# Three 64-byte gaps in SBUF between the operand tiles of a LayerNorm, attention and FFN kernel

## The chip, the cores and the metric

The kernel runs on one core of one Trainium2 chip. The metric is the device time of one launch in microseconds (us). The engines are named as the profile names them: PE is TensorE's matmul side, PEld its loading of the stationary operand, DVE is VectorE, ACT is ScalarE, POOL is GpSimd, and SPq is the queue of SyncE, from which all transfers are issued.

## What is computed

The input x is 16 x 1024 x 256 in float32. It is normalised over its last dimension (no scale, no shift), and two branches are added to x:

```python
xn = _layernorm(x, axis=-1)
x = x + attention(xn, Wqkv, Wout) + ffn(xn, W1, b1, W2, b2)
# attention: 16 heads of 16; segments of 512 tokens; every 8th token is a key (64 keys);
#   scores minus their maximum over each block of 64 queries, exp,
#   num = w @ v, den = sum(w) + 1e-10, out = num / den, then @ Wout.T
# ffn: relu(xn @ W1 + b1) @ W2 + b2, inner width 1024
```

## The kernel before

The 16 x 1024 tokens are 32 segments of 512. The program is software pipelined: while the hidden layer of segment s is computed, the queries, keys and scores of segments s+1 and s+2 are made. Each engine has its own instruction stream, and a loop over 14 pairs of segments stands between written-out first and last steps.

To keep float32 accuracy with fp32r products, each operand is split in a high and a low part, and `three_products` (L990 to L996) adds hi x hi, lo x hi and hi x lo in PSUM. Each of the three is a pair of a load of the stationary operand (128 x 128) and a product that streams a moving operand of 128 partitions by 512 columns of 4 bytes. Three such products are made for each of the following, in every segment unless it is said otherwise.

- `first_product`: stationary a slice of `w1_hi`/`w1_lo`, moving `xt_hi`/`xt_lo` (normalised x, transposed), output `h_bank`: 8 slices of the inner width times 2 halves of the depth, so 48 products.
- `second_product`: stationary `w2_hi`/`w2_lo`, moving `h_hi`/`h_lo`, output `y_bank`: 48 products. In the very last segment the roles are exchanged (stationary a slice of h, moving 256 columns of w2).
- `queries`: stationary `wq`, moving `xt`: 12 products.
- `output_product`: stationary `wout`, moving `att_hi`/`att_lo`: 12 products.
- `keys_values`: stationary `xkey_hi`/`xkey_lo`, moving `wkv`: 6 products for each pair of segments.

Outside `three_products` there are three more kinds. `scores` (L1063) makes one product for each of 8 pairs of heads, stationary `k_pack`, moving `q_pack`, 96 partitions. `weighted_values` (L1159) makes 32 small ones, stationary `v` (64 partitions by 32 columns), moving `w_exp` (512 columns); eight of them lie side by side in the array. The transposes have `xn_keys`, `kv` or `xn` as stationary and `identity` as moving operand, 128 columns.

The streams of the other engines follow PE. ACT and DVE take PSUM out and split it (ACT writes `h_hi` and `h_full` at L603 and L605, `xt_hi` at L642; DVE writes `xt_lo`, `q_lo` and the shifted scores), POOL makes `h_lo` (L524) and `att_lo`. SP issues all transfers in one fixed order: among others the blocks of x to memory and back (L421, L427), the outputs to memory and back (L438, L444), the keys to memory (L354, L357) and back in `k_pack` (L364), the queries in `q_pack` (L372 waits for `q_lo`, L374 issues). The first `scores` of a segment waits for `q_pack` and `k_pack`.

The tiles are laid out in SBUF in the order in which `sb(...)` is called, each starting at the next multiple of 32 bytes of a partition. In this layout the start of every operand of the products above leaves the remainder 96 when divided by 128: the weights (`w1_hi` starts at byte 35552), `xt` (99296), `xkey`, `q_hi`, `v` (144352), `k_pack` (150496), `q_pack` (125920), `w_exp` (154848), `att_hi` and `h_hi` (204512), and also `xn`, `xn_keys` and `kv`. The one exception is `identity` (16512), with the remainder 0. Slices inside the tiles start at multiples of 128 bytes from there. `y_mem` is the last tile and ends at byte 229088 of the 229376 of a partition.

Of the kernel before, what the change touches and what calls it, by code (L numbers as in the profile page):

```python
# [22 lines left out]
F32 = mybir.dt.float32  # L23
# [5 lines left out]
P = 128  # L29
# [19 lines left out]
def ln_attention_ffn(nc, x, wq_t, wkv_t, wout_t, w1, b1, w2, b2, out):  # L49
# [19 lines left out]
    with ExitStack() as ctx:  # L69
        def sb(name, shape, dt):  # L70
            return ctx.enter_context(nc.sbuf_tensor(name, shape, dt))
# [15 lines left out]
        w1s = [sb(f"w1_{n}", [P, DH, INTER], F32R) for n in ("hi", "lo")]  # L87
        w2s = [sb(f"w2_{n}", [P, NH, D], F32R) for n in ("hi", "lo")]

        x_raw = sb("x_raw", [P, 2, T, D], F32)  # L90
        x_keys = sb("x_keys", [P, D], F32)
        x_b2 = sb("x_b2", [P, 2, T, D], F32)
# [16 lines left out]
        v = sb("v", [P, 2, PAIRS, PW], F32)  # L109
        k_full = sb("k_full", [P, 2, DH, P], F32)  # L110
        k_part = [sb(f"k_{n}", [P, DH, P], F32R) for n in ("hi", "lo")]
        k_pack = sb("k_pack", [P, PAIRS // 2, DH, P], F32R)
        k_dram = nc.dram_tensor("k_dram", [2, PAIRS // 2, PW, DH * P], F32).ap()
        s_max = sb("s_max", [P, PAIRS, NB], F32)
# [5 lines left out]
        den_dram = nc.dram_tensor("den_dram", [P // PW, 2, QUADS, SEG], F32).ap()  # L120
        rden_dram = nc.dram_tensor("rden_dram", [P // PW, 2, QUADS, SEG], F32).ap()
        att = sb("att", [P, QUADS, SEG], F32)
        att_part = [sb(f"att_{n}", [P, QUADS, SEG], F32R) for n in ("hi", "lo")]
        h_full = sb("h_full", [P, HBUF, SEG], F32)
        h_part = [sb(f"h_{n}", [P, HBUF, SEG], F32R) for n in ("hi", "lo")]
# [1141 lines left out]
```

## Time and profile before

| what | us |
|---|---|
| median of 3 runs | 1087.76 |
| lowest and highest of them | 1080.11 and 1087.91 |
| the profiled execution | 1080.21 |
| its span, first to last instruction | 1078.4 |

The profiled execution is one launch on the chip; its own time is 1.8 us above its span, and it lies at the low end of the runs. Durations and starts of instructions are taken from it. Busy time of PE counts overlapping products once, and since products are pipelined one in the row is shown longer (0.39 us) than the distance to the next one (about 0.23 us). The distance between starts is what a product costs.

### The profile page before, as it was taken

The numbers are of one execution on the slowest core, as the hardware profiler recorded it, in microseconds if no ns is written. First come the engines' busy times: TensorE is split into PE (matmuls) and PEld (weight loads), VectorE is DVE, ScalarE is ACT, GpSimd is POOL, SyncE is SP. The second block draws the span as 40 slices with busy tenths as digits, with TensorE's granted clock in tenths as the row PEclk, the third lists the DMA queues.
The fourth block names the chain that finished last, engine by engine and source line by source line (L and its number), as shares of the span: only waits on it lengthen the run. The fifth ranks groups of instructions, "written<-read, shape, count | busy, mean of one in ns | idle before, by whom it ended". The sixth has DMA issues, their size and how long they took to land.

```text
span 1078.4 us, 19171 instructions
## 1 busy us (share of the span) xinstructions
PE 1047.4 (97%) x5381; PEld 813.1 (75%) x5381; DVE 818.8 (76%) x1464; ACT 647.9 (60%) x1080; POOL 622.7 (58%) x487
## 2 busy tenths in 40 slices
PE   5899999999999999999999999999999999999996
PEld 4577787777787777787777787777787777777775
DVE  7787877877877877877877777877877877878632
ACT  5656665666666566665656656566665666655651
POOL 5255565656565665565655655665565656556562
PEclk9999999999999999999999999999999999999999
DMA  5357777787877777777687887777777787866733
GB/s 190 97 154 206 221 210 212 191 233 197 234 223 192 199 214 219 225 213 209 185 234 197 231 224 191 197 215 219 221 209 217 186 229 199 242 192 182 192 108 117
DMA packets 153287, 216.37 MB, mean 201 GB/s; under 512 B 27312, under 2 KB 96432, under 8 KB 153264
## 3 DMA queue, kind: packets, MB, share of 16 engines
q1 hardware_dynamic: 153264, 216.09, 72.3%
q8 instruction: 12, 0.20, 0.1%
q14 instruction: 11, 0.09, 0.0%
HBM read 100.41 MB, written 58.46 MB: 147 GB/s over the span
## 4 chain that ended last, share of the span: by engine, by line
PE 86%; DMA 6%; DVE 3%; SPq 3%; issue 2%; ACT 1%; POOL 0%; POOLq 0%; DVEq 0%; ACTq 0%
PE h_bank L994 36%; PE y_bank L994 36%; PE s_banks L1063 5%; PE misc L1159 3%; PE s_banks L1159 2%; PE misc L994 2%; DMA k_dram<-k_lo 2%; DMA yt_dram<-y_mem 1%; SPq L399 1%; DVE xn L805 1%; DMA xt_dram<-z 1%; DMA k_pack<-k_dram 1%; SPq L438 1%; DVE s_max L822 0%; SPq L421 0%
## 5 line engine op out<-in xcount | busy, mean ns | idle before, releaser
L524 POOL TENSOR_TENSOR h_lo<-h_full,h_hi 128x512 fp32r<-128x512 f32 x256 | 335.8, 1312 | 394.0 <-ACT h_full L605 384.0
L611 ACT ACTIVATE w_exp<-w_exp 128x512 f32<-128x512 f32 x256 | 161.5, 632 | 245.8 <-DVE w_exp L828 243.9
L603 ACT ACTIVATE h_hi<-h_bank,b_cols 128x512 fp32r<-128x512 f32 x256 | 174.5, 682 | 71.2 <-PE h_bank L994 63.9
L994 PE MATMUL h_bank<-xt_hi,w_hi 128*128 128x512 f32 x512 | 206.9, 404 | 0.0
L994 PE MATMUL h_bank<-xt_lo,w_hi 128*128 128x512 f32 x512 | 200.7, 392 | 0.0
L994 PE MATMUL h_bank<-xt_hi,w_lo 128*128 128x512 f32 x512 | 200.2, 391 | 0.0
L994 PE MATMUL y_bank<-h_hi,w_hi 128*128 128x512 f32 x496 | 194.9, 393 | 1.6 <-ACT w_exp L611 1.6
L822 DVE TENSOR_REDUCE s_max<-s_banks 128x8 f32<-128x512 f32 x254 | 170.9, 673 | 33.2 <-PE s_banks L1063 33.0
L994 PE MATMUL y_bank<-h_lo,w_hi 128*128 128x512 f32 x496 | 194.0, 391 | 0.0
L994 PE MATMUL y_bank<-h_hi,w_lo 128*128 128x512 f32 x496 | 193.7, 391 | 0.0
L828 DVE TENSOR_TENSOR w_exp<-s_banks,s_max 128x512 f32<-128x512 f32 x254 | 175.7, 692 | 11.0
L605 ACT ACTIVATE h_full<-h_bank,b_cols 128x512 f32<-128x512 f32 x256 | 174.4, 681 | 0.0
L994 PEld LDWEIGHTS h_bank<-xt_hi,w_hi 128*128 128x128 f32 x512 | 96.2, 188 | 47.2 <-issue 27.1
L994 PEld LDWEIGHTS h_bank<-xt_hi,w_lo 128*128 128x128 f32 x512 | 96.4, 188 | 21.0
L994 PEld LDWEIGHTS y_bank<-h_hi,w_hi 128*128 128x128 f32 x496 | 93.6, 189 | 22.2 <-issue 2.0
L994 PEld LDWEIGHTS h_bank<-xt_lo,w_hi 128*128 128x128 f32 x512 | 96.6, 189 | 17.9
L994 PEld LDWEIGHTS y_bank<-h_lo,w_hi 128*128 128x128 f32 x496 | 93.7, 189 | 20.5
L994 PEld LDWEIGHTS y_bank<-h_hi,w_lo 128*128 128x128 f32 x496 | 93.2, 188 | 20.6
L941 DVE STREAM_TRANSPOSE y_mem<-y_bank 128x512 f32<-128x512 f32 x62 | 44.4, 717 | 77.8 <-PE y_bank L994 77.8
L1063 PE MATMUL s_banks<-q_pack,k_pack 96*128 96x512 f32 x248 | 95.2, 404 | 3.3 <-DMA k_pack<-k_dram 1.6
L536 POOL TENSOR_TENSOR att_lo<-att,att_hi 128x512 fp32r<-128x512 f32 x62 | 78.7, 1290 | 23.8 <-ACT att_hi L616 23.7
L531 POOL TENSOR_TENSOR att<-num_den,rden_rows 128x512 f32<-128x512 f32 x62 | 84.3, 1382 | 5.3 <-DMA rden_rows<-rden_dram 4.8
(135 smaller groups left out, 1513.5 us busy)
## 6 DMA issues: line engine op xcount, KB each, us to landing
q_pack<-q_hi SPq DMA_DIRECT2D x248, 128.0 KB, 2.5
x_raw<-x SPq DMA_DIRECT2D x32, 512.0 KB, 4.8
rden_rows<-rden_dram SPq DMA_DIRECT2D x128, 128.0 KB, 4.6
x_b<-x SPq DMA_DIRECT2D x32, 512.0 KB, 4.5
q_pack<-q_lo SPq DMA_DIRECT2D x124, 128.0 KB, 2.4
yt_dram<-y_mem SPq DMA_DIRECT2D x124, 128.0 KB, 3.6
y_mem<-yt_dram SPq DMA_DIRECT2D x31, 512.0 KB, 4.6
out<-x_b SPq DMA_DIRECT2D x31, 512.0 KB, 3.1
```

What stands on the lines that cost most here:

```text
L524: pool.tensor_tensor(h_part[1][:, i % HBUF], h_full[:, i % HBUF], f32(h_part[0][:, i % HBUF]), ALU.subtract).then_inc(h_lo, 1)
L531: pool.tensor_tensor(att[:, quad], num_den[:, quad, 0], rden_rows[:, quad], ALU.mult).then_inc(att_ready, 1)
L536: pool.tensor_tensor(att_part[1][:, quad], att[:, quad], f32(att_part[0][:, quad]), ALU.subtract).then_inc(att_lo, 1)
L603: act.activation(h_part[0][:, i % HBUF], h_bank[i % 2][:], ACT.Relu, bias=b1_cols[:, i:i + 1]).then_inc(h_hi, 1)
L605: act.activation(h_full[:, i % HBUF], h_bank[i % 2][:], ACT.Relu, bias=b1_cols[:, i:i + 1]).then_inc(h_ready, 1)
L611: act.activation(w_exp[:, pair], w_exp[:, pair], ACT.Exp).then_inc(w_ready, 1)
L822: dve.tensor_reduce(s_max[:, pair], ps.rearrange("p t n i -> p n t i"), AX.XY, ALU.max).then_inc(max_ready, 1)
L828: dve.tensor_tensor(w_exp[:, pair].rearrange("p (t n i) -> p t n i", t=T, n=NB), ps, top, ALU.subtract).then_inc(s_shifted, 1)
L941: dve.transpose(y_blocks[:, :, a].rearrange("p i t n -> p t i n"), y_bank[a][:].rearrange("p (t i n) -> p t i n", t=T, n=PW)).then_inc(y_r ...
L994: mm = pe.matmul(ps, stationary[a], moving[b], start=start and c == 0 and n == 0, stop=stop and c == len(pairs) - 1 and n == 2, skip_group ...
L1063: pe.matmul(s_bank[n % 2], k_pack[0:PR, pair % (PAIRS // 2), pair // (PAIRS // 2)], q_pack[0:PR, pair], start=True, stop=True).then_inc(s_ ...
L1159: mm = pe.matmul(pv_banks[quad][PW * j:PW * (j + 1), a], v[rows, 1 - par, pair], w_exp[rows, pair], start=True, stop=True)
```

## The change

Three tiles of 16 floats (64 bytes in each partition) that nothing reads or writes are put between others. All tiles behind the first gap move up by 64 bytes, those behind the second by 128, those behind the third by 192. No instruction is added, removed or moved.

```diff
         w2s = [sb(f"w2_{n}", [P, NH, D], F32R) for n in ("hi", "lo")]
 
+        sb("gap_weights", [P, 16], F32)
         x_raw = sb("x_raw", [P, 2, T, D], F32)
...
         k_part = [sb(f"k_{n}", [P, DH, P], F32R) for n in ("hi", "lo")]
+        sb("gap_keys", [P, 16], F32)
         k_pack = sb("k_pack", [P, PAIRS // 2, DH, P], F32R)
...
         att = sb("att", [P, QUADS, SEG], F32)
+        sb("gap_rows", [P, 16], F32)
         att_part = [sb(f"att_{n}", [P, QUADS, SEG], F32R) for n in ("hi", "lo")]
```

The remainders by 128 become: weights 96 as before; from `x_raw` to `k_lo` (so `xt`, `xkey`, `q_hi`, `q_pack`, `kv`, `v`, `xn`, `xn_keys`) 32; from `k_pack` to `att` (so `k_pack`, `w_exp`) 96; from `att_hi` on (`att_hi`, `h_full`, `h_hi`, `h_lo`, `y_mem`) 32; `identity` stays at 0. The last byte used becomes 229280.

## Rows read from the trace of the kernel before

**Rows 1.** Head of the page: span and busy time of each engine
```profile
span 1078.4 us, 19171 instructions
...
PE 1047.4 (97%) x5381; PEld 813.1 (75%) x5381; DVE 818.8 (76%) x1464; ACT 647.9 (60%) x1080; POOL 622.7 (58%) x487
```

**Rows 2.** The chain that ended last: share of the span by engine
```profile
PE 86%; DMA 6%; DVE 3%; SPq 3%; issue 2%; ACT 1%; POOL 0%; POOLq 0%; DVEq 0%; ACTq 0%
```

**Rows 3.** Groups of PE: form, count | busy us, mean ns | idle before
```profile
L994 PE MATMUL h_bank<-xt_hi,w_hi 128*128 128x512 f32 x512 | 206.9, 404 | 0.0
...
L994 PE MATMUL y_bank<-h_hi,w_hi 128*128 128x512 f32 x496 | 194.9, 393 | 1.6 <-ACT w_exp L611 1.6
...
L1063 PE MATMUL s_banks<-q_pack,k_pack 96*128 96x512 f32 x248 | 95.2, 404 | 3.3 <-DMA k_pack<-k_dram 1.6 <-DVE w_exp L828 1.0 <-DMA q_pack<-q_hi 0.5
L994 PE MATMUL h_bank<-xt_hi,wq_hi 128*128 128x512 f32 x124 | 48.7, 392 | 0.1
...
L994 PE MATMUL y_bank<-att_hi,wout_hi 128*128 128x512 f32 x124 | 48.2, 389 | 0.0
...
L994 PE MATMUL misc<-wkv_hi,xkey_hi 128*128 128x512 f32 x30 | 11.8, 392 | 1.6 <-issue 1.6
```

**Rows 4.** Stretch of the full pipeline: us, busy (count), PEclk, DMA share, GB/s
```profile
35.00:1040.00 1005.00, 996.20 (x5101) 770.94 (x5099) 780.77 (x1389) 615.65 (x1031) 590.46 (x458) 1.00 0.75 206
```

**Rows 5.** Timeline of PE in mid-span: start us, us, line, operation, out<-in
```profile
521.63 0.39 PE L994 MATMUL h_bank<-xt_lo,w_hi 128*128 128x512 f32 x1
...
525.26 0.39 PE L994 MATMUL y_bank<-att_hi,wout_lo 128*128 128x512 f32 x1
```

**Rows 6.** Timeline of PE from a scores product on
```profile
530.13 0.40 PE L1063 MATMUL s_banks<-q_pack,k_pack 96*128 96x512 f32 x1
530.37 0.40 PE L994 MATMUL y_bank<-h_hi,w_hi 128*128 128x512 f32 x1
530.60 0.40 PE L994 MATMUL y_bank<-h_lo,w_hi 128*128 128x512 f32 x1
530.84 0.39 PE L994 MATMUL y_bank<-h_hi,w_lo 128*128 128x512 f32 x1
531.07 0.39 PE L994 MATMUL y_bank<-h_hi,w_hi 128*128 128x512 f32 x1
531.29 0.39 PE L994 MATMUL y_bank<-h_lo,w_hi 128*128 128x512 f32 x1
```

**Rows 7.** Granted clock of a stretch, PE and PEld in it
```profile
48.00:51.00 3.00, 3.00 (x9) 2.32 (x8) 2.96 (x8) 1.01 (x3) 0.00 (x0) 0.50 0.93 201
```
```profile
48.28 0.63 PE L994 MATMUL h_bank<-xt_lo,w_hi 128*128 128x512 f32 x1
...
50.84 0.63 PE L994 MATMUL y_bank<-h_hi,w_hi 128*128 128x512 f32 x1
```
```profile
49.14 0.33 PEld L994 LDWEIGHTS h_bank<-xt_lo,w_hi 128*128 128x128 f32 x1
```

**Rows 8.** PEld beside the stretch of rows 5
```profile
522.77 0.19 PEld L994 LDWEIGHTS y_bank<-att_lo,wout_hi 128*128 128x128 f32 x1
523.00 0.19 PEld L994 LDWEIGHTS y_bank<-att_hi,wout_lo 128*128 128x128 f32 x1
```

**Rows 9.** Timeline of PE: two sets of the weighted values
```profile
518.49 0.64 PE L1159 MATMUL misc<-w_exp,v 64*32 64x512 f32 x8
518.92 1.06 PE L1159 MATMUL s_banks<-w_exp,v 64*32 64x512 f32 x16
```

**Rows 10.** Waits of PE and of the queue: us in total, times, longest
```profile
PE s_banks L1063 <- DMA k_pack<-k_dram: 1.6, 3, 1.0
```
```profile
SPq L372 <- DVE q_lo L871: 43.9, 31, 3.4
```

**Rows 11.** Last segment, 256 columns moving: timeline of PE
```profile
1044.88 0.28 PE L994 MATMUL y_bank<-w_hi,h_hi 128*128 128x256 f32 x1
...
1045.85 0.28 PE L994 MATMUL y_bank<-w_hi,h_lo 128*128 128x256 f32 x1
```

## The prediction

> **What bounds the kernel now.** I read the head of the page first: PE is busy 97% of the span, DVE 76%, all others less [rows 1]. The chain that ended last is PE for 86% [rows 2], and in the 1005 us of the full pipeline PE is busy 996 us at the full granted clock [rows 4]. So PE sets the time, and the idle time before its groups is a few us in all [rows 3]. The change adds no instruction; it can act only through how fast the same instructions run. The question is whether a product takes longer than its columns need, and whether that surplus depends on where the operands lie.
>
> The timeline answers the first half. In mid-span 16 distances between starts, which cross three kinds of products, take 525.26 - 521.63 = 3.63 us, so 226.9 ns each [rows 5]. What the same 512 columns need is shown by a stretch in which the clock is granted at half, the lower of the two levels (1.2 instead of 2.4 GHz): six distances take 50.84 - 48.28 = 2.56 us, so 426.7 ns [rows 7]. Half of that is 213.3 ns. At full clock each product thus carries a surplus of 13.5 ns that the half clock does not show, though in both a load of 128 columns runs beside it: 0.33 us at half clock [rows 7], 0.19 us at full clock [rows 8]. A fixed cost of exchanging the stationary operand in array cycles would have doubled at half clock; it is gone. A surplus that appears only when the moving operand is read at full pace, with a second read of SBUF beside it, looks like the two reads getting in each other's way.
>
> Two further places speak for a surplus that depends on how the two reads stand to one another. With 256 moving columns eight distances take 1045.85 - 1044.88 = 0.97 us, 121 ns, against 106.7 for the columns alone, so about the same surplus of 14 ns for a product of half the length [rows 11]: it goes with the load, which is the same, not with the columns. And after every scores product (96 partitions instead of 128) four distances take 531.07 - 530.13 = 0.94 us, 235 ns each, before they fall back to 0.22 or 0.23 [rows 6]; the instructions are of the same form as those of rows 5, with the same remainder 96. The same pair of reads can cost 13 or 22 ns, so something about their relative position counts. That it is the address by 128 bytes is what no row shows: all these products have operands of the same remainder.
>
> **The change part by part.** The gaps themselves cost nothing: no instruction touches them, and the last tile still ends inside the partition. Since each gap is 64 bytes and the tiles start at multiples of 32, starts by 64 bytes are what they were; I take the price for transfers and for DVE, ACT and POOL as 0. They are off PE's path (76, 60 and 58% busy, [rows 1]); bounds are plus or minus 1% of the 1005 us if they did react, since DVE at 76% hides more than that.
>
> All three gaps have one effect on PE, so they are summed together. Full-width products: three each of the forms with 512, 496, 124, 124 and 30, and 248 scores, so 3 x 1286 + 248 = 4106 [rows 3]. Their surplus now: 4106 x 13.5 ns = 55.4 us, and four distances after each of the 248 scores by a further 8 ns (235 - 226.9), 7.9 us. Together 63 us of the 1080.2 us depend on how the reads meet.
>
> What is left of it with operands half of 128 bytes apart is unknown; I bound it from both sides. The low end is nothing left, -63 us, by the half-clock distance [rows 7]. The high end is the position shown after scores, 235 ns for all: the 4106 - 992 = 3114 products that are not there yet pay 8 ns more, +25 us [rows 6]. The nearest row for products whose two reads do not meet at full pace is that of the weighted values, where eight tiles of 32 columns share the array and stream 512 columns in 518.92 - 518.49 = 0.43 us [rows 9], 3 ns above 426.7. I take 3 ns as what stays of a product, so the gain is 63 - 4106 x 3 ns = 63 - 12 = 51 us.
>
> The Trainium skill gives a price for that remainder (TensorE: Matmul & The Clock Gate, "Wait — 56ns, not 53.3ns?"): about 2.5 ns a product at full clock, 215.7 ns for 512 columns. The trace's 226.9 ns disagrees with it by 11 ns for these 4-byte operands; by the page the gain would be about 53 us.
>
> Not all of it arrives. 51 us over 31 segments is 1.6 us a segment. SP waits for the low part of the queries 43.9 us over 31 times, so 1.4 us in the mean [rows 10]: that is the slack of the queue ahead of the copies that the next scores need, and the same place already stops PE three times, 1.6 us together. Beyond the slack PE waits for the queue: 31 x (1.6 - 1.4) = 6, with the uneven slack I take 7 us. It would be late as the first scores of a segment waiting for `k_pack`, not for `q_pack`. Bounds: 0 if the queue gets earlier with PE, since much of what it waits for is PE's work; 20 us if in every second segment, the ones that repack keys, over 1 us is lost.
>
> Transposes keep a stationary operand that is not a multiple of 128 away from `identity` (96 before, 32 after), and the score products of the very first segment have both operands at 32; together below 1 us, at 0. The weighted values also get opposite halves, but already run within 3 ns of their columns: 0.
>
> Sum: 1080.2 - 51 + 7 = 1036 us. This is against the profiled execution, which is at the low end of the three runs (median 1087.8); other runs after the change may read up to 7 us more.
>
> **The rivals.**
>
> *Nothing happens.* The surplus belongs to the pair of reads whatever their addresses, for example because a load takes turns at a read path which the moving operand fills only at full clock. For it: the stretch of rows 5 crosses three kinds of products, whose operands lie kilobytes apart, at one even distance, so higher address bits do not matter and the low ones may not either [rows 5]. Against it: the 235 ns after scores. Time: 1080 to 1088 us. The Trainium skill speaks against the change here (TensorE: Matmul & The Clock Gate, step 1 of "Step-by-step: what each phase is for"): loading the next tile's weights does not take read bandwidth from the running product. This trace contradicts it as far as time goes, since 13.5 ns go somewhere, but the rule would leave the change at 1080.
>
> *Part of it.* The moving read covers 2048 bytes a product and the load 512, at different pace, so the one overtakes the other's place by 128 bytes several times wherever they start. Another start saves only some of the meetings: half of the 55 us, 27 us, with no give-back below the slack: 1053 us.
>
> *Slower.* The present alignment is the good one. In steady state the distances fall back to 226.9 by themselves after each disturbance, so this is a settled state, and the disturbed one costs 235. If opposite halves put every pair permanently in the disturbed position, all 4106 products run at 235 ns: 1080 + 25 = 1105 us. It decides at `three_products`, and from the point at which the distance in the stretch of rows 5 exceeds 229.5 ns (11 us of 4106 products) it is slower than 1%.
>
> **How the numbers follow.** The full removal 0.36, part of it 0.13, nothing 0.29, slower 0.22. A measurement of this kernel tells about 1% (11 us) from no change. Faster by over 1% is the first two, 0.49; same 0.29; slower 0.22. The likeliest one's own range is 1017 (nothing left) to 1056 (the 51 us with 20 us given back and the 7 us of spread). The range of all has to take in part of it and nothing as well, up to 1095 with a little of the slower case; it leaves out most of the 0.22. Below, full removal with no give-back is 1017; I put 1019.
>
> **What would show it.** Right: the distance in the stretch of rows 5 falls to 213 to 218 ns, the disturbance after scores to under 4 ns, the half-clock distance stays 426.7, PEld's mean stays near 188 ns, DVE's share rises to about 79%, and waits of scores for `k_pack` appear in more than three segments. If the distance is still 226.9 the first rival holds; at 218 to 224 the second; at 230 or more the third. Wrong in another way: the distances fall and the span does not, with the waits of PE grown by as much; or the distances of one form change and of others not, which would mean that it is not the halves of 128 bytes that count but another address bit.

## The result, and the profile after

The kernel with the gaps takes 1093.15 us (median of 9 runs, 1092.10 to 1096.98), the kernel before 1084.63 us (median of 9, 1080.11 to 1087.91). The ratio is 1.0096, with a 95% interval of 1.0078 to 1.0114. The gaps make the kernel about 1% slower, where 4 to 5% faster was forecast. The profiled execution took 1092.1 us, with a span of 1090.3 us, 11.9 us longer than that of [rows 1]; the mean granted clocks of the two are 0.995 and 0.997. The clock is not the reason: the mean granted clock of these nine runs is 0.990 to 0.995, and that of the 57 runs of the kernel before that stand beside the experiments is 0.987 to 0.995.

The head of the page of the changed kernel, and the shares of its chain:

```profile
span 1090.3 us, 19171 instructions
...
PE 1060.4 (97%) x5381; PEld 814.5 (75%) x5381; DVE 815.9 (75%) x1464; ACT 649.0 (60%) x1080; POOL 622.3 (57%) x487
...
PE 93%; DVE 2%; issue 2%; DMA 2%; SPq 1%; POOL 1%; ACT 0%; POOLq 0%; DVEq 0%; ACTq 0%
```

The instructions are as many as before, and DVE, ACT and POOL are busy for the same time as in [rows 1], within 0.4%. Only PE has more busy time, by 1060.4 - 1047.4 = 13.0 us, and its share of the chain is larger than in [rows 2]. What of the span PE is not busy has not grown: 29.9 us, where it was 31.0. So PE waits no more than before; PE itself is slower. One view says this without a sum: a stretch in which PE is never idle. The same 200 us of mid-span, first of the kernel before, then of the changed one (columns: stretch, us; busy us and count of PE, PEld, DVE, ACT, POOL; granted clock; DMA share; GB/s):

```profile
300.00:500.00 200.00, 200.00 (x1020) 155.97 (x1019) 157.37 (x283) 123.72 (x208) 118.32 (x93) 1.00 0.77 211
```
```profile
300.00:500.00 200.00, 200.00 (x1009) 154.07 (x1008) 153.83 (x277) 121.17 (x203) 119.14 (x94) 1.00 0.72 207
```

PE is busy for all 200 us in both, at the full granted clock, and the gaps leave it 1009 recorded products where it had 1020: 1.1% fewer. The busy share cannot show such a loss; the count can, roughly, since a trace can lack some records.

The timeline of the changed kernel in the place of [rows 5] shows which products pay. First six distances of the first FFN product, then eleven of the output product:

```profile
526.59 0.39 PE L997 MATMUL h_bank<-xt_hi,w_lo 128*128 128x512 f32 x1
...
527.96 0.39 PE L997 MATMUL h_bank<-xt_hi,w_lo 128*128 128x512 f32 x1
528.19 0.40 PE L997 MATMUL y_bank<-att_hi,wout_hi 128*128 128x512 f32 x1
...
530.76 0.39 PE L997 MATMUL y_bank<-att_hi,wout_lo 128*128 128x512 f32 x1
```

With `xt` moving the distance is (527.96 - 526.59) / 6 = 228 ns, with `att_hi` moving it is (530.76 - 528.19) / 11 = 234 ns, and before both were at 226.9 ns [rows 5]. Both pairs lie half of 128 bytes apart, yet they differ. What tells them apart is the sign, an inference here that the experiments take up: `xt` starts 64 bytes above the weights (by the remainder), `att_hi` 64 bytes below them, counted as 160 against 224 in remainders of 256.

After a scores product, in the place of [rows 6]:

```profile
535.62 0.40 PE L1066 MATMUL s_banks<-q_pack,k_pack 96*128 96x512 f32 x1
535.85 0.40 PE L997 MATMUL y_bank<-h_hi,w_hi 128*128 128x512 f32 x1
...
536.55 0.39 PE L997 MATMUL y_bank<-h_hi,w_hi 128*128 128x512 f32 x1
```

Four distances take 0.93 us, 232.5 ns each. These products run at that level now anyway, so the disturbance of [rows 6] is no longer an extra cost.

Where the clock is granted at half, nothing has changed:

```profile
47.75 0.63 PE L997 MATMUL h_bank<-xt_lo,w_hi 128*128 128x512 f32 x1
...
50.31 0.63 PE L997 MATMUL y_bank<-h_hi,w_hi 128*128 128x512 f32 x1
```

Six distances take 2.56 us as in [rows 7], 426.7 ns each. The waits of PE for the keys, in the place of [rows 10]:

```profile
PE s_banks L1066 <- DMA k_pack<-k_dram: 1.0, 1, 1.0
```

One wait instead of three, which fits a slower PE that gives the queue more time. The starts of all recorded products of 512 columns, taken together, account for the loss. What the distances between 212 and 245 ns have above 213.3 ns sums up to 61.1 us before and 74.1 us after. That is 13.0 us more, as much as PE's busy time has grown; the span is 11.9 us longer.

### The profile page after: what moved, and what is told of

Its sections match the earlier page's. It is cut to its first block, busy times and chain, and to the rows that moved or that the text cites. A ratio compares the mean times of both kernels' runs of the same rounds, so it can differ in the third digit from the quotient of the medians.

```text
span 1090.3 us, 19171 instructions
## 1 busy us (share of the span) xinstructions
PE 1060.4 (97%) x5381; PEld 814.5 (75%) x5381; DVE 815.9 (75%) x1464; ACT 649.0 (60%) x1080; POOL 622.3 (57%) x487
## 4 chain that ended last, share of the span: by engine, by line
PE 93%; DVE 2%; issue 2%; DMA 2%; SPq 1%; POOL 1%; ACT 0%; POOLq 0%; DVEq 0%; ACTq 0%
PE h_bank L997 40%; PE y_bank L997 39%; PE s_banks L1066 5%; PE misc L1162 3%; PE s_banks L1162 2%; PE misc L997 2%; DVE xn L808 0%; DMA k_dram<-k_lo 0%; DMA yt_dram<-y_mem 0%; DMA x_raw<-x 0%; PE misc L1128 0%; PE misc L1111 0%; SPq L402 0%; PE s_banks L1077 0%; DMA xt_dram<-z 0%
```

## The experiments

Theory one: the surplus of a product depends on the distance between the starts of its moving and stationary operand, and the kernel before had the best one, zero. Its rivals: the surplus depends on where each operand starts by itself; it has to do with other tiles that the gaps moved, read by DVE, ACT, POOL or DMAs; it goes with the volume of the stationary load. A second question was the period: 128 bytes, as the prediction thought, or another. The expectations give their theories letters of their own, explained there. The three kernels with products alone ran once each, the others in several rounds beside the kernel before, whose medians in them are 1083.94, 1084.68 and 1084.07 us.

**The products alone, one pair of starts after the other.** The whole computation is left out; 24 products follow each other for each pair of starts, and nothing else runs.

```diff
+for g, (_, m, s, n) in enumerate(groups()):
+    for r in range(24):
+        mm = pe.matmul(banks[g % 2][:, 0:n], stat[:, s:s + P], mov[:, m:m + n], start=True, stop=True)
```

> A kernel of fp32r products alone, 24 in a row for each pair of starts: the moving operand is shifted by 4 to 512 bytes against a fixed stationary one, then both together by 16 to 112 bytes, then the stationary one alone, then with 384, 320 and 256 columns. It leaves out the whole computation. Theory A (the distance of two starts depends on moving start minus stationary start, modulo 128): the distance goes from 226.7 ns at 0 to about 233 ns at 64 bytes and comes back at 128, 256 and 384; shifting both together changes nothing. Theory B (the sum goes by the absolute place of one operand): shifting both by 64 gives 233 ns too, and shifting only the stationary one differs from the mirror image. Theory C (address makes no difference to PE and something else in the kernel slowed it): 226.7 ns everywhere. If some shift reaches 213 to 216 ns there is a layout that beats both kernels.

The timeline of this kernel; each row is one group of 24 products, so the start of the next group less its own start, divided by 24, is the distance. The groups are shifts of the moving operand of 0, 4, 20, 28, 64, 128 and 192 bytes, each shown with the row behind it, then the stationary operand alone by 64 bytes, and 256 columns at 0:

```profile
24.30 5.60 PE L71 MATMUL bankb<-mov,stat 128*128 128x512 f32 x24
29.74 5.84 PE L71 MATMUL banka<-mov,stat 128*128 128x512 f32 x24
35.41 5.75 PE L71 MATMUL bankb<-mov,stat 128*128 128x512 f32 x24
...
52.06 5.92 PE L71 MATMUL banka<-mov,stat 128*128 128x512 f32 x24
57.81 5.77 PE L71 MATMUL bankb<-mov,stat 128*128 128x512 f32 x24
63.42 5.60 PE L71 MATMUL banka<-mov,stat 128*128 128x512 f32 x24
68.86 5.76 PE L71 MATMUL bankb<-mov,stat 128*128 128x512 f32 x24
...
113.45 5.66 PE L71 MATMUL bankb<-mov,stat 128*128 128x512 f32 x24
118.94 5.83 PE L71 MATMUL banka<-mov,stat 128*128 128x512 f32 x24
...
202.78 5.76 PE L71 MATMUL bankb<-mov,stat 128*128 128x512 f32 x24
208.38 5.76 PE L71 MATMUL banka<-mov,stat 128*128 128x512 f32 x24
...
225.19 5.75 PE L71 MATMUL bankb<-mov,stat 128*128 128x512 f32 x24
230.78 5.79 PE L71 MATMUL banka<-mov,stat 128*128 128x512 f32 x24
...
391.74 5.76 PE L71 MATMUL bankb<-mov,stat 128*128 128x512 f32 x24
397.34 5.77 PE L71 MATMUL banka<-mov,stat 128*128 128x512 f32 x24
...
418.31 3.04 PE L71 MATMUL bankb<-mov,stat 128*128 128x256 f32 x24
421.18 2.99 PE L71 MATMUL banka<-mov,stat 128*128 128x256 f32 x24
```

Read from these rows: 5.44 / 24 = 226.7 ns at 0, 236 at 4 bytes, 240 at 20, 227 at 28, 228.8 at +64, 233.3 at 128, 233 at 192. The settled distances (the mean of the last twelve of each group) in a table, in ns:

| moving start less stationary start, bytes | 0 | 4 | 8 | 12 | 16 | 20 | 24 | 28 | 32 | 64 | 96 | 128 | 160 | 192 | 240 | 256 |
|---|---|---|---|---|---|---|---|---|---|---|---|---|---|---|---|---|
| distance | 226.7 | 236.7 | 233.3 | 228.9 | 231.7 | 240.0 | 233.3 | 226.7 | 233.3 | 228.8 | 233.3 | 233.3 | 234.3 | 233.3 | 226.7 | 226.7 |

Shifts of 272, 320 and 384 bytes give the same as 16, 64 and 128 within 1 ns: the period is 256 bytes, and theory A of the expectation, with 128, is wrong in its period. No shift is below 226.7. Both operands shifted together by 32, 64 or 96 bytes stay at 226.7, and the stationary operand alone shifted by 64 gives 5.60 / 24 = 233.3, the value of -64 (192 in the table). So for a stationary start at a multiple of 32 bytes, as all tiles here have, it is the difference that counts, and its sign too. At finer steps the difference is not all: shifts of both by an odd multiple of 16 give 230.0, and in the second kernel of this kind a stationary start 16 bytes off gives another table, with 226.7 at a difference of 64 and 228.8 at 192. With 256 columns the distance is 2.87 / 24 = 120 ns: the surplus is again about 13 ns.

**One gap in front of everything.** All operands move by 64 bytes, their differences stay.

```diff
+sb("gap_front", [P, 16], F32)
 identity = sb("identity", [P, P], F32)
```

> One gap of 64 bytes in front of all tiles, so that every operand moves by 64 bytes and no difference between operands changes (remainder 32 for all, identity 64). Theory A: same as before, ratio 1.000 within 0.003, distances of 226.7 ns in the stretch of rows 5. Theory B: slower, as after, ratio 1.007 to 1.012.

Ratio 1.0004 (0.9974 to 1.0033), median 1083.71 us, and the sum of the distances above 213.3 ns is 60.8 us, beside 61.1 before. Where the tiles lie by themselves does not matter at this step of 64 bytes, within 0.3% for the whole kernel and 0.3 us for PE's distances. The rival of single places is out. The rival of other tiles loses its ground too: the products alone show the same distances with nothing else running, and the busy times of the other engines did not grow with the gaps.

**The third gap alone.** Only `att` and `h` parts move against the weights, by +64 bytes.

```diff
+sb("gap_rows", [P, 16], F32)
 att_part = ...
```

> Only the third gap (64 bytes before the halves of the attention rows): att, h_hi, h_lo lie opposite the weights, xt, queries, keys and values as before. Theory A: only the second product and the output product (60 of 131 full-width products of a segment) rise to about 233 ns and the first product and the queries stay at 226.7 except next to them; 31 segments x 60 x 6.6 ns = 12 us more minus what the disturbed products after scores cost already: ratio 1.004 to 1.010. Theory D (only the keys, queries and scores matter, through the gaps at the keys): ratio 1.000.

Ratio 1.0032 (1.0013 to 1.0051), median 1088.45 us. By the table 3 x (496 + 124) = 1860 products pay 2.1 ns, an estimate of 4 us; the medians differ by 4.5, less than the 0.4 to 1.0% that was expected from 233 ns. The sum of the distances grows by 6.1 us. The products of `h` and `att` stand at 230.5 ns in the mean, above the 228.8 of the table, and those of `xt`, whose starts have not changed and which stand between them, rise from 227.8 to 229.0 ns in the mean: a product's distance depends on its neighbours as well.

**The gaps at 32, 96 and 32 bytes.** `xt` against the weights gets +32, `h` and `att` get 160, both poor in the table.

```diff
-sb("gap_weights", [P, 16], F32)
+sb("gap_weights", [P, 8], F32)
...
-sb("gap_keys", [P, 16], F32)
+sb("gap_keys", [P, 24], F32)
...
-sb("gap_rows", [P, 16], F32)
+sb("gap_rows", [P, 8], F32)
```

> The same three places, with gaps of 32, 96 and 32 bytes: moving minus stationary is 32 instead of 64 bytes (modulo 128). If the cost grows with the distance of the halves, between before and after: ratio 1.003 to 1.008. If 128 bytes are eight places of 16 and each shift has a settled state of its own, anything from 0.96 to 1.03; the scan at 32 bytes tells which, and the kernel must follow it: each ns of the distance is 4.1 us.

Ratio 1.0136 (1.0114 to 1.0159), median 1099.22 us, slower than the change, and the sum of the distances is 19.9 us above that of the kernel before. By the table 1908 products at 6.6 ns and 1950 at 7.6 ns would pay 27 us, less some 7 us that the products behind scores paid already, so about 20, an estimate. The loss follows the table.

**One gap of 128 bytes behind the weights.** If the period were 128 bytes, nothing would change.

```diff
+sb("gap_weights", [P, 32], F32)
 x_raw = ...
```

> One gap of 128 bytes behind the weights: all remainders by 128 are as in the kernel before, those by 256 differ by 128 between weights and moving operands. Theory M128 (the difference counts modulo 128, as the change supposes): ratio 1.000. Theory M256 (it counts modulo 256, as in the scan, 233.3 ns at 128): 3858 products outside the scores pay 6.7 ns more, 26 us, minus up to 7 us of disturbance that is in that level already: ratio 1.016 to 1.025.

Ratio 1.0131 (1.0105 to 1.0156), median 1098.37 us. The timeline of this kernel, eleven distances of the output product:

```profile
533.56 0.40 PE L995 MATMUL y_bank<-att_hi,wout_hi 128*128 128x512 f32 x1
...
536.13 0.40 PE L995 MATMUL y_bank<-att_hi,wout_lo 128*128 128x512 f32 x1
```

2.57 / 11 = 234 ns, the value of the scan at 128. The period of 128 bytes is out. The loss is below the 1.6 to 2.5% that was expected, and less than the table alone gives: 3858 products by 6.6 ns are 25 us. The four products behind each scores product already paid their 8 ns before [rows 6], which takes off 992 x 6.6 ns = 6.5 us; the sum of the distances has grown by 15.7 us, and what is missing to 19 stays open.

**The first gap alone.** The products of `xt`, `h` and `att` all get +64. Of the full-width products only those of the keys and values, 90 in all, get -64, since `wkv` lies in front of the gap; the scores keep 0.

```diff
+sb("gap_weights", [P, 16], F32)
 x_raw = ...
```

> The first gap alone (64 bytes behind the weights): moving minus stationary is +64 bytes in the first and second product, queries and output product, where the change has +64 for xt and -64 for h and att. By the scan +64 costs 228.8 ns and -64 (192) 233.3 ns: 3858 x 2.2 ns = 8 us, less the part that hides in the disturbance after scores: ratio 1.003 to 1.008, so faster than the change (1.0096). If the sign doesn't count, the same as the change or more: 1.010 or above.

Ratio 1.0051 (1.0031 to 1.0072), median 1089.95 us: about half of the change's loss, although here too every operand of `three_products` lies half of 128 bytes from its partner. The sum of the distances grows by 5.8 us instead of 13.0. The sign that the two levels of the changed kernel's timeline suggested is confirmed by the total.

**The products alone in other forms.** The whole computation is left out again; each group varies one property at shift 0 unless it is said otherwise.

```diff
-mm = pe.matmul(banks[g % 2][:, 0:n], stat[:, s:s + P], mov[:, m:m + n], start=True, stop=True)
+mm = pe.matmul(banks[g % 2][0:cols, 0:n], w, x_, start=True, stop=True)
```

> Products alone again, 24 in a row for each form; the whole computation is left out. Theory F (the surplus over 213.3 ns is the load's read of SBUF meeting the moving read): with 96, 64 and 32 stationary columns the surplus of 13.3 ns shrinks in proportion to about 10, 7 and 3 ns; with the stationary operand read from one element only (step 0) or the moving one from one element only it changes and no longer depends on the start; bf16 operands, half the bytes, come near 215 to 217 ns at any shift. Theory G (the surplus is a fixed cost of an fp32r product): 13.3 ns in all of these. Theory H (96 partitions disturb): one product of 96 partitions among 11 of 128 gives 232.5, 237.5, 232.5, 231 ns behind it and then 226.7, and all of 96 partitions in a row give 226.7. The shifts repeat the scan: 228.8 at 64 bytes, 233.3 at 128 and 192, 226.7 at 256, 233.3 at 384, 233.3 at 768 minus a multiple of 256 and so on; with the stationary start 16 bytes off, another table of the same kind, nowhere below 226.

The timeline of this kernel, with 96, 64 and 32 stationary columns, 96 and 64 partitions, then a moving operand of step 0 (one column read over and over), both operands of step 0, and bf16 at shift 64:

```profile
20.64 5.69 PE L97 MATMUL banka<-mov,stat 128*96 128x512 f32 x24
26.17 5.68 PE L97 MATMUL bankb<-mov,stat 128*64 128x512 f32 x24
31.68 5.72 PE L97 MATMUL banka<-mov,stat 128*32 128x512 f32 x24
37.24 5.62 PE L97 MATMUL bankb<-mov,stat 96*128 96x512 f32 x24
42.80 5.75 PE L97 MATMUL banka<-mov,stat 64*128 64x512 f32 x24
...
88.39 5.41 PE L97 MATMUL bankb<-mov,stat 128*128 128x512 f32 x24
93.63 5.41 PE L97 MATMUL banka<-mov,stat 128*128 128x512 f32 x24
...
104.08 5.34 PE L97 MATMUL banka<-mov_b,stat_b 128*128 128x512 bf16 x24
109.26 5.34 PE L97 MATMUL bankb<-mov_b,stat_b 128*128 128x512 bf16 x23
```

A load of a quarter of the columns does not shrink the surplus; the settled distance even rises, to 231.7 ns with 32 columns. The rival of the load's volume is out. A moving operand of step 0 takes 5.24 / 24 = 218 ns, while a stationary operand of step 0 with a normal moving one takes 231.7: some 8 of the 13 ns go when the moving read stands still, and none when the stationary read does. And bf16 takes 5.18 / 24 = 216 ns, at shifts of 0, 64 and 128 bytes alike: the surplus above 216 is one of the 4-byte operands. Of the two theories of the expectation neither holds as it stands, F because fewer columns do not shrink the surplus, G because it is not the same in all forms.

**Scores over 128 partitions.** Rows 96 to 127 of `k_pack` and `q_pack` are set to zero once, so that the scores products have the form of all others. Does the disturbance of [rows 6] go, and does the time follow?

```diff
+pool.memset(f32(k_pack[PR:P]).rearrange("p a b c -> p (a b c)"), 0.0).then_inc(pads_made, 1)
...
+pool.memset(f32(q_pack[PR:P]).rearrange("p a b -> p (a b)"), 0.0).then_inc(pads_made, 1)
...
-pe.matmul(s_bank[n % 2], k_pack[0:PR, ...], q_pack[0:PR, pair], ...
+pe.matmul(s_bank[n % 2], k_pack[0:P, ...], q_pack[0:P, pair], ...
```

> The layout before, but the scores are made over 128 partitions, with rows 96 to 127 of both operands zero (set once at the start by POOL). Theory H: the disturbance after each of the 248 scores goes (6 + 11 + 6 + 4 = 27 ns each, 6.7 us in all), all distances of the inner loop are 226.7 ns, ratio 0.993 to 0.996; what may be given back is a wait of the first scores for their transfers. If the disturbance is due to the exchange of tiles and not to the 96 partitions: ratio 1.000 and 232, 237, 232, 231 ns as before.

Ratio 0.9994 (0.9976 to 1.0012), median 1083.32 us. The timeline behind a scores product, and the waits for the keys, of this kernel:

```profile
530.67 0.39 PE L1069 MATMUL s_banks<-q_pack,k_pack 128*128 128x512 f32 x1
...
531.58 0.39 PE L1000 MATMUL y_bank<-h_hi,w_hi 128*128 128x512 f32 x1
```
```profile
PE s_banks L1069 <- DMA k_pack<-k_dram: 4.6, 7, 0.9
```

Four distances take 0.91 us, 227.5 ns each where [rows 6] had 235: the disturbance is gone, and the summed surplus falls by 5.5 us. But the waits of PE for `k_pack` grow from three to seven, from 1.6 us to 4.6 us [rows 10], and the median falls by little more than 1 us, which the interval does not tell from none and which misses the expected 0.993 to 0.996. This is the give-back that the prediction costed, met at a gain of a tenth of its size: PE gets ahead of the copies that bring the keys. The two profiled executions must not be compared by their spans, since their mean granted clocks differ: 0.990 in this one, 0.997 in that of the kernel before.

**The keys ahead of the output rows.** In each step SP sends the keys to memory before it fetches the rows of `y_mem`, so that the copies that the next scores need are earlier.

```diff
+if norm:
+    keys_to_dram(s)
 ...
-    keys_to_dram(s)
```

> The layout before, but SP sends the keys to memory ahead of fetching the outputs back (512 KB), so that the repacking of the keys is not queued behind that fetch. If the first scores' wait for k_pack is what takes up to 1 us in every second segment: the three to four such waits go, the runs no longer spread to 1088, ratio 0.995 to 1.000. If the fetch of the outputs becomes late instead, DVE's sum of the residual holds up its transposes and then PE: ratio above 1.002.

Ratio 0.9974 (0.9961 to 0.9987), median 1080.88 us, and the runs spread less: 1078.67 to 1082.41, beside 1080.62 to 1088.42 of the kernel before in the same rounds. The profile does not say where this comes from: PE still waits twice for `k_pack`, 1.3 us together, where [rows 10] had three times and 1.6 us, so the waits did not go as expected.

**Both together, and the gaps with the keys ahead.** The first joins the last two edits; the second joins the three gaps with the earlier keys, to see whether the loss of the gaps stands when the queue is no longer in the way.

```diff
+if norm:
+    keys_to_dram(s)
 ...
+pe.matmul(s_bank[n % 2], k_pack[0:P, ...], q_pack[0:P, pair], ...
```

> Both: scores over 128 partitions, and the keys ahead of the outputs. If the 5.5 us that the scores over 128 partitions took from the distances of PE came back as waits for k_pack, they stay now: ratio 0.990 to 0.995, faster than both kernels. If another wait takes them: 0.998 to 1.001 as without the reordering.

```diff
+sb("gap_weights", [P, 16], F32)
+sb("gap_keys", [P, 16], F32)
+sb("gap_rows", [P, 16], F32)
 ...
+if norm:
+    keys_to_dram(s)
```

> The change's three gaps together with the keys ahead of the outputs. The gaps' cost to PE's distances is 13 us in the two profiles; with the wait for k_pack out of the way in both, it shows in full: 13 us above the same kernel without gaps, which is ratio 1.012 over it and 1.007 to 1.012 over the kernel before. If the gaps cost something beside PE's distances the difference is larger than 15 us.

Both together: 0.9929 (0.9907 to 0.9952), median 1076.87 us, faster than the kernel before and the changed one. The wait for the keys is back to where it was before the scores were widened:

```profile
PE s_banks L1070 <- DMA k_pack<-k_dram: 1.7, 3, 0.7
```

The gaps with the keys ahead: 1.0080 (1.0060 to 1.0100), median 1093.09 us. Against the same kernel without gaps that is 12.2 us, 1.1%, and the summed surplus is 74.1 us against 60.3. In its profile PE waits for `k_pack` once, for 0.2 us. So the loss of the gaps is PE's own; with the keys earlier the medians show nearly all of the 13.8 us, where those of the change show 8.5 of 13.0, a difference that is near the spread of the runs.

**The products alone: what stays from one group to the next.** The whole computation is left out once more; a group of shift 0 stands between groups of other starts.

```diff
+for d in (1, 5, 9, 16, 32, 48):
+    out += [one(f"moving shifted by {4 * d}", d, 0), base]
+out += [one("moving 0, stationary 16, behind base", 0, 4), one("both 16", 4, 4), ...,
+        one("both 112", 28, 28), one("moving 0, stationary 16, behind both 112", 0, 4), base]
```

> Products alone, 24 in a row for each form; the whole computation is left out. Open is what the surplus belongs to. Theory R (it is paid once a product by the moving read, and the load only decides the phase): with 448, 384, 320 and 256 columns it stays 13.3 ns a product at start 0, and also at 128 bytes it stays near 20 ns instead of shrinking; with the moving operand read from one element it is 5 ns and no stationary start changes that; with the stationary operand from one element or with 32 columns the start of the moving one still counts. Theory S (settled states with a memory): the base form comes back to 226.7 ns behind every disturbance, but the form with the stationary start 16 bytes off settles at 226.7 ns behind the base and at 233.3 ns behind the form where both are 112 bytes off. Theory J (the surplus is the jump of the moving read from its end back to its start): a moving operand that goes on where the last ended gives 215 to 220 ns.

The timeline of this kernel: the same pair of starts (stationary operand shifted by 16 bytes) first behind the group of shift 0, then behind one with both operands shifted by 112 bytes; then the moving operand of step 0 with the stationary one shifted by 128 bytes; then one that goes on where the last product ended, three times in four:

```profile
94.47 5.60 PE L97 MATMUL bankb<-mov,stat 128*128 128x512 f32 x24
99.91 5.68 PE L97 MATMUL banka<-mov,stat 128*128 128x512 f32 x24
...
116.48 5.76 PE L97 MATMUL bankb<-mov,stat 128*128 128x512 f32 x24
122.07 5.63 PE L97 MATMUL banka<-mov,stat 128*128 128x512 f32 x24
...
143.29 5.41 PE L97 MATMUL banka<-mov,stat 128*128 128x512 f32 x24
148.54 5.41 PE L97 MATMUL bankb<-mov,stat 128*128 128x512 f32 x24
...
262.38 5.60 PE L97 MATMUL banka<-mov,stat 128*128 128x512 f32 x24
267.82 5.60 PE L97 MATMUL bankb<-mov,stat 128*128 128x512 f32 x24
```

The same pair of starts runs at 5.44 / 24 = 226.7 ns in one place and at 5.59 / 24 = 233 ns in the other, and stays there for the whole group: a pair can have two settled distances, and what ran before chooses (theory S). At shift 0 this was never seen; every group of shift 0 came back to 226.7 within ten products, whatever had gone ahead. With a moving operand of step 0 the stationary start does not matter: 5.25 / 24 = 219 ns at 128 bytes, as at 0. Nor does the moving start with a stationary operand of step 0: 231.1 to 231.7 ns at all five starts tried, where theory R expected it to count. So the starts count only where both reads advance, which speaks for the two reads getting in each other's way; how they do it stays open. A moving read that jumps back only after every fourth product stays at 226.7, so the jump is not what costs, and theory J is out. At shift 0 the surplus is 13.3 ns with 512, 384, 320 and 256 columns, but 20.0 with 448; at 128 bytes it falls from 20.0 ns with 512 columns to 12.4 with 256.

## Why the prediction was wrong, step by step

**PE sets the time: right.** The whole loss appears in PE's distances, in the stretch with 1009 products where 1020 were, and the other engines' busy times moved by less than 0.4%.

**The surplus of 13.5 ns belongs to a product, whatever its length: right in the main.** At shift 0 it is 13.3 ns with 512, 384, 320 and 256 columns, though 20.0 with 448, and it is gone at half clock with the gaps as without.

**It depends on how the two operands start to one another: right, and shown** by the front gap (nothing) against the single gaps (3 and 5 thousandths) and by the scan.

**"I take 3 ns as what stays of a product": the step that failed.** It makes the 51 us of the forecast. The row behind it was that of the weighted values [rows 9], 64 partitions and eight tiles side by side, whose distance was read as the absence of a meeting between the reads. That reading does not hold by the prediction's own numbers. The 426.7 ns with which it compares the 0.43 us are the distance at half clock, but the row was taken at the full granted clock [rows 4], where 512 columns need 213.3 ns; a set of eight takes twice that, and no run tells why. Nor is the 0.43 us the distance of every set. The row of both sets of a longer stretch starts at 518.04:

```profile
518.04 1.09 PE L1159 MATMUL misc<-w_exp,v 64*32 64x512 f32 x16
```

The set that starts there takes 518.49 - 518.04 = 0.45 us. And the operands are not of the type of the full-width ones: the program declares `w_exp` and `v` as F32, the full-width ones as F32R. So the row gives no price for a full-width fp32r product. What the runs show instead is a surplus of 15.5 ns (228.8) for pairs at +64 and 20 ns (233.3) for pairs at -64, and never less than 13.3 ns for these operands at any shift tried. The 13.5 ns of the kernel before were not a penalty of a bad alignment but the lowest that any pair of starts tried gave for full-width products of this type. By the table the change costs 3 x (512 + 124) = 1908 products by 2.1 ns and 3 x (496 + 124 + 30) = 1950 products by 6.6 ns, 4 + 13 = 17 us, less what products behind scores had already paid; measured were 13.0 us in the distances. (The 248 scores are at -64 now too, and rise from 232.8 to 234.1 ns in the mean, 0.3 us.)

**The price for 512 columns.** The Trainium skill (TensorE: Matmul & The Clock Gate, "Wait — 56ns, not 53.3ns?") puts a product of 512 columns at 215.7 ns. The bf16 groups agree, at 215.8; the 4-byte products do not, at 226.7 and above. The prediction set this price beside its 3 ns, though by its own words [rows 5] had contradicted it by 11 ns for the type at hand; that row, and not the 3 ns, was the one to go by.

**Distance by 128 bytes: wrong.** The gap of 128 bytes costs 1.3%; the period is 256. In remainders of 256 the change produced two cases, not one. The prediction had named this sign: distances of one form that change otherwise than those of another mean that another address bit counts.

**The rival "slower" held, with about half of its size.** Its reason was that distances fall back to 226.9 by themselves after each disturbance, "so this is a settled state", and it does: shift 0 always comes back. But a settled distance need not be the lowest, since 128 bytes settle too, at 233.3 ns; that 226.7 is the lowest is what the scan found, and the rival could not know it. Its price took 235 ns for all, +25 us; the products with `xt` moving went only to 228 ns in the stretch shown and 230.3 in the mean of the whole trace, and the products of `h` behind scores lost nothing more (233.6 ns in the mean before, 232.8 after). Its deciding point of 229.5 ns over 4106 products is 11 us, and the 13.0 us of the distances lie just above it, at the border of 1%.

**"Nothing" and "part of it": wrong.** The even distance over operands kilobytes apart [rows 5] spoke for "nothing", but all those pairs had difference 0 by 256, so the row could not tell.

**Give-back of 7 us for the keys: not put to the test by the change,** since PE never got ahead. The kernel with scores over 128 partitions shows it: 5.5 us less in the distances, 3.0 us of them in new waits for `k_pack`, a good 1 us in the median. **Gaps at no cost for DVE, ACT, POOL and DMAs: right,** by the front gap and by their busy times with the three gaps. **Nothing for the weighted values: right,** their sets start 453, 429 and 429 ns apart with the gaps as without.

## What to carry to other kernels

In a kernel bound by PE with 4-byte operands, let the moving and the stationary tile of a product start at the same remainder by 256 bytes, the best that was found here for tiles at multiples of 32 bytes; a careless tile size in front of one of them can cost over 1%, and no busy share shows it, only distances between starts or the number of products in a full stretch. A surplus above the ideal is not yet a loss that can be had back: look for a row of the same form and type that lacks it, and where there is none, let a small scan of the operation alone come first. And before a layout is changed, find out what the present one is in the period that counts, for it may be the best one already.

## What the runs showed of the hardware that was not expected

- With the stationary start at a multiple of 32 bytes, the distance between full-width fp32r products of 512 columns depends on the difference of the two starts by 256 bytes, between 226.7 ns (0, 28, 240) and 240.0 ns (20), and differs with the sign: 228.8 ns at +64, 233.3 at -64. With bf16 it was 215.8 ns at all three shifts tried.
- The worst differences are no multiples of 16 bytes: 236.7 ns at 4 bytes, 240.0 at 20 (236.2 behind another group), against 234.5 at most for multiples of 16.
- One product of 96 partitions among those of 128 slows the next four by 8 ns each [rows 6]; 96 partitions in every product run at 226.7 ns, so it is the change of form that disturbs. A moving operand of step 0, alone the fastest of the 4-byte forms at 218 ns, disturbs too: put in for one product in twelve it takes 215 ns itself and is followed by seven distances of 224 to 236 ns before they settle at 226.7 again.
- Two settled distances for one pair of starts, 226.7 and 233.3 ns, chosen by what ran before.
- Products of 32 partitions, one behind the other with nothing else, ran at a lower granted clock. The windows of the kernel with the other forms, during the group of 64 partitions, that of 32, and the group behind it (one product of 96 partitions in twelve, the others of 128):

```profile
43.00:48.00 5.00, 5.00 (x23) 4.01 (x23) 0.00 (x0) 0.00 (x0) 0.00 (x0) 1.00 0.00 0
49.00:57.00 8.00, 8.00 (x22) 6.10 (x22) 0.00 (x0) 0.00 (x0) 0.00 (x0) 0.57 0.00 0
58.00:65.00 7.00, 7.00 (x20) 5.42 (x20) 0.00 (x0) 0.00 (x0) 0.00 (x0) 0.59 0.01 2
```

PE is busy throughout all three, yet the granted clock is 1.00 with 64 partitions and 0.57 with 32: nearly the whole of that stretch at the lower of the two levels, 1.2 GHz. It stayed there for most of the next group, 0.59, though all but two of its products have 128 partitions. What made it fall was not followed up.
